# A transformer block: the preparation of cross attention placed inside self attention and the first cross steps

## What is computed

```python
attn_in = _adaln(x, cond, ln1_w, ln1_b, g1_w, g1_b, b1_w, b1_b)
x = _attn(attn_in, attn_in, sa_wq, sa_wkv, sa_wo, sa_bo) + x
cross_in = _adaln(x, cond, ln1_w, ln1_b, g1_w, g1_b, b1_w, b1_b)
ctx_n = _ln(context, ca_lnc_w, ca_lnc_b)
x = _attn(cross_in, ctx_n, ca_wq, ca_wkv, ca_wo, ca_bo) + x
```

## Time and profile before

| | us |
|---|---|
| median of 3 runs | 2244.72 (2241.64 to 2246.07) |
| the profiled execution | 2244.09 |
| its span, first to last instruction | 2242.2 |
| self attention, to the first transfer of `prepare` | 1555.25 |
| `prepare` and `project_context` | 90.07 |
| cross attention, from its first transfer at 1645.32 to its end at about 2037.3 | 392.0 |
| feed-forward | 204.9 |

### The profile page before, as it was taken

One profiled execution on the slowest core, in us unless ns is written; L12 is line 12 of the kernel. 1 busy time (PEld: TensorE's weight loads), 2 busy tenths in 40 slices (PEclk: granted clock), 3 DMA queues, 4 the chain that ended last, 5 costly groups with the idle time before them and its releaser, 6 DMA issues. The chain is left out here.

```text
span 2242.2 us, 40840 instructions
## 1 busy us (share of the span) xinstructions
PE 2056.6 (92%) x16376; PEld 932.5 (42%) x16376; DVE 1794.6 (80%) x2801; ACT 1378.4 (61%) x1748; POOL 35.0 (2%) x26
## 2 busy tenths in 40 slices
PE   4799999999999999999999999997379999986999
PEld 2233333345333335433333533335233444444676
DVE  5888999986899997799999689965768888844654
ACT  4577777765777766677677476762547666633442
POOL 1000000000000000000000000000400000000000
PEclk8799999999999999999999999998589999987999
DMA  5010101111110100111110111003323343324111
GB/s 189 29 39 30 48 30 58 40 39 42 55 39 30 67 37 23 61 45 39 39 39 30 48 59 38 30 20 97 91 81 116 111 124 125 120 73 130 38 39 38
DMA packets 102116, 136.04 MB, mean 61 GB/s; under 512 B 36694, under 2 KB 75176, under 8 KB 101928
## 3 DMA queue, kind: packets, MB, share of 16 engines
q1 hardware_dynamic: 101927, 133.43, 18.2%
HBM read 67.89 MB, written 13.11 MB: 36 GB/s over the span
## 5 line engine op out<-in xcount | busy, mean ns | idle before, releaser
L943 ACT ACTIVATE sa_probs<-sa_ps_s 128x1024 f32<-128x1024 f32 x512 | 496.3, 1021 | 216.1 <-PE sa_ps_s L734 216.1
L749 PE MATMUL sa_ps_o<-sa_probs,sa_v_pair 128*64 128x512 f32 x2048 | 530.9, 610 | 7.4 <-DVE sa_mx L1085 7.4
L1098 DVE TENSOR_TENSOR sa_acc<-sa_acc,sa_probs 128x1024 f32<-128x1024 f32 x384 | 452.7, 1220 | 16.5 <-ACT sa_probs L943 8.2
L1085 DVE CUSTOM_DVE_ANT_0 sa_rise<-sa_ps_t,sa_rise 128x512 f32<-128x512 f32 x504 | 327.1, 686 | 133.9 <-PE sa_ps_t L711 131.1
L931 ACT ACTIVATE sa_rise<-sa_ps_t 128x1024 f32<-128x1024 f32 x252 | 257.4, 1022 | 156.3 <-PE sa_ps_t L704 156.1
L727 PE MATMUL sa_ps_s<-sa_hi 64*128 64x512 f16 x1024 | 197.0, 377 | 0.9 <-ACT sa_raw L917 0.9
L727 PE MATMUL sa_ps_s<-sa_lo,sa_hi 64*128 64x512 f16 x1024 | 197.0, 377 | 0.0
L727 PE MATMUL sa_ps_s<-sa_hi,sa_lo 64*128 64x512 f16 x1024 | 196.8, 377 | 0.0
L749 PEld LDWEIGHTS sa_ps_o<-sa_probs,sa_v_pair 128*64 128x64 f32 x2048 | 114.7, 135 | 164.6 <-issue 96.4
L704 PE MATMUL sa_ps_t<-sa_kd,sa_hi 64*128 64x512 f16 x504 | 99.8, 390 | 33.2 <-ACT sa_raw L917 19.9
L704 PEld LDWEIGHTS sa_ps_t<-sa_kd,sa_hi 64*128 64x128 f16 x504 | 26.1, 93 | 216.6 <-issue 173.5
(11 more groups left out here) (329 smaller groups left out, 4020.7 us busy)
## 6 DMA issues: line engine op xcount, KB each, us to landing
sa_swp<-sa_raw SPq DMA_DIRECT2D x124, 256.0 KB, 2.4
sa_inv<-sa_scratch SPq DMA_DIRECT2D x128, 128.0 KB, 2.9
ca_swp<-ca_raw SPq DMA_DIRECT2D x64, 256.0 KB, 2.4
ca_inv<-ca_scratch SPq DMA_DIRECT2D x64, 256.0 KB, 3.9
sa_xs<-in_x SPq DMA_DIRECT2D x4, 1024.0 KB, 5.8
sa_xr<-in_x SPq DMA_DIRECT2D x4, 1024.0 KB, 5.8
cap_xs<-x_after_self SPq DMA_DIRECT2D x4, 1024.0 KB, 6.9
x_after_cross<-ca_xr SPq DMA_DIRECT2D x32, 128.0 KB, 2.0
```

What stands on the lines that cost most here:

```text
L749: ins = pe.matmul(ps_o[rows(x), half(c)], v_pair[:, kt, rows(x)], probs[:, kt % 2, c, half(x)], start=(kt == 0), stop=(kt == NK - 1))
L943: act.activation(probs[:, kt % 2, c, :], ps_s[c][:, :], ACT.Exp, scale=float(DH) ** -0.5).then_inc(s_p, 1)
L1085: dve.tensor_tensor_reduce(out=larger, in0=max_banks(j, t)[:, half(x)], in1=larger, scale=1.0, scalar=-3.0e38, op0=ALU.add, op1=ALU.max, a ...
L1098: dve.tensor_tensor(acc[:, c, :], before, probs[:, kt % 2, c, :], ALU.add).then_inc(s_acc[c], 1)
```

## The change

`prepare`, `project_context` and the function that clears semaphores are gone. Their work goes to four places.

- The loop of self attention: three more norms, u = 4, 5 and 6, for batches 0, 1 and 2 of x1, which are read back once they are stored. Norms 2 and 3 move to earlier steps. In the steps 30 and 31 and after the loop the cross weights are loaded into buffers that have come free (`later`) and converted (`following_high`, `following_low`).
- The beginning of self attention: the context is loaded, normalised, turned and split.
- The prologue of cross attention: `context_keys` and `context_values` on PE, `evacuate_keys`, `evacuate_values` and `high_keys` on ACT, `turned_keys` and `low_keys` on DVE.
- The first cross steps: the norm of batch 3, with statistics in steps 1 to 4, the inverse root in step 5, the normalising in steps 6 and 7 and the turning in steps 7 to 10.

The scale and shift (`gam`, `bet`) of self attention are kept and used again. `raw`, `hi`, `lo` and other buffers of the two attentions now share memory: `raw_or_keys` was `raw`, `scores_or_weights` holds `hi` and `lo` of self attention and then the cross weights, `context_or_sums` holds `cT` and then `sums`.

```diff
-def clear_semaphores(nc, sems):
...
-def prepare(nc, tag, consts, x_src, cond, norm, weights, xT_hi, xT_lo, context=None):
...
-def self_attention(nc, consts, x_src, x_dst, cond, norm, weights, bo, xT, wq, wk, wv, wo):
+def self_attention(nc, consts, x_src, x_dst, cond, norm, weights, bo, xT, wq, wk, wv, wo, shared, context, following):
...
-    NORMS = {1: (0, 1), 2: (8, 2), 3: (16, 3)}
+    NORMS = {1: (0, 1), 2: (5, 2), 3: (10, 3), 4: (16, 0), 5: (21, 1), 6: (28, 2)}
+    CROSS_NORMS = 4
...
+                if u >= CROSS_NORMS:
+                    sp.wait_ge(s_out, 16 * (norm_batch(u) + 1))
+                source = y_v if u >= CROSS_NORMS else x_v
+                sp.dma_start(xs[:], source[norm_batch(u)]).then_inc(s_nx, 16)
+            def stage_following(n):
+                src = following[n][0]
+                dst = later[n][0:src.shape[0]]
+                if len(src.shape) == 3:
+                    dst = dst.rearrange("p (a b) -> p a b", b=src.shape[2])
+                sp.dma_start(dst, src).then_inc(s_fw[n // 2], 16)
...
             sp.dma_start(ropeS[:], consts["sines"]).then_inc(s_rope, 16)
+            sp.dma_start(cs[:], c_src.rearrange("b m d -> m b d")).then_inc(s_c, 16)
+            sp.dma_start(crow[:, 0, :], c_w.partition_broadcast(M)).then_inc(s_c, 16)
+            sp.dma_start(crow[:, 1, :], c_b.partition_broadcast(M)).then_inc(s_c, 16)
                 swap(0, i)
+            sp.wait_ge(s_nlo, 4)
             stage(6)
             stage(7)
...
                     line(g + 1)
+                if g == G - 3:
+                    for i in (1, 0):
+                        sp.wait_ge(s_kq[i], 2 * G)
+                        for n in range(2):
+                            stage_following(2 * (1 - i) + n)
+                if g == G - 1:
+                    sp.wait_ge(s_v, 2 * G)
+                    for n in (4, 5):
+                        stage_following(n)
+                    sp.wait_ge(s_ntr, 4 * (len(NORMS) + 1))
+                    for n in (6, 7):
+                        stage_following(n)
...
+            def context_transposes():
+                pe.wait_ge(s_cn, 3)
+                for k, height, dst in c_parts:
+                    for b in range(B):
+                        ins = pe.transpose(dst[:, b * M:(b + 1) * M], cs[:, b, k * P:k * P + height], ident[0:M, 0:M])
+                    ins.then_inc(s_ct, 1)
...
+                if t == TT - 2:
+                    pe.wait_ge(s_kq_r[0], 4)
+                    context_transposes()
...
                     if norm_bank(g, kt) is not None:
                         u, n = norm_bank(g, kt)
                         pe.wait_ge(s_nxc, TT * (u + 1))
+                        if j == G:
+                            pe.wait_ge(s_v_r, 2 * G)
+                            pe.wait_ge(s_nxn, 4 * u + n)
                         transposes(u, n)
...
+                if t == 4:
+                    pe.wait_ge(s_nxn, 4 * (len(NORMS) + 1))
...
+            def following_high(n):
+                src, w_hi, _ = following[n]
+                height = src.shape[0]
+                act.wait_ge(s_fw[n // 2], 32)
+                act.activation(w_hi[0:height], later[n][0:height], ACT.Copy, scale=WS).then_inc(s_fhi, 1)
...
+            act.wait_ge(s_cst, 3)
+            act.activation(c_root[:], c_var[:], ACT.Sqrt).then_inc(s_croot, 1)
...
+                    if g == G - 2 and kt in (1, 3):
+                        if kt == 1:
+                            act.wait_ge(s_lo[0], G)
+                            act.wait_ge(s_lo[1], G)
+                        following_high(kt // 2)
...
+            act.wait_ge(s_st, NK * G)
+            for n in range(2, len(following)):
+                following_high(n)
...
+            context_variances()
             dve.wait_ge(s_rope, 32)
...
             weights_low(5)
+            context_norm()
             for t in range(TT):
...
                 rotated(1, i)
+            for n in range(2):
+                context_low(n)
             low(1, 1)
...
+                    if g == G - 2 and kt in (2, 4):
+                        n = kt // 2 - 1
+                        following_rest(n)
+                        following_low(n)
             reciprocals(G - 1)
+            dve.wait_ge(s_st, NK * G)
+            for n in range(2, 5):
+                following_rest(n)
+                following_low(n)
             for c in range(2):
...
-def project_context(nc, consts, cT, wk, wv, hi, lo, v_all):
...
-def cross_attention(nc, consts, x_src, x_dst, bo, xT, k_hi, k_lo, v_all, wq, wo):
...
+    STATS, NORMALISE, TRANSPOSE = range(1, 5), (6, 7), range(7, 11)
...
-            sp.dma_start(xr[:], x_v[0]).then_inc(s_x_first, 16)
             sp.wait_ge(s_blo, 1)
             sp.dma_start(bo_rows[1:2, :], bo_low[1:2, :]).then_inc(s_brow, 16)
+            for n in range(2):
+                sp.wait_ge(s_cev, PH * (n + 1))
+                sp.dma_start(k_half(k_swp, n)[0:P:2], k_half(k_raw, n)[1:P:2]).then_inc(s_kswap[n], 16)
+                sp.dma_start(k_half(k_swp, n)[1:P:2], k_half(k_raw, n)[0:P:2]).then_inc(s_kswap[n], 16)
             swap(0)
+            sp.dma_start(xs[:], x_v[LAST]).then_inc(s_nx, 16)
             swap(1)
+            sp.wait_ge(s_cpr, 2 * PAIRS)
+            sp.dma_start(xr[:], x_v[0]).then_inc(s_x_first, 16)
             for g in range(G):
                 if g + 2 < G:
                     swap(g + 2)
...
+            def context_keys(pair):
...
+            def context_values(n):
...
+            def transposes(n):
+                pe.wait_ge(s_nxc, TT if n else TT // 2)
...
+                if (b, pair, c) == (LAST, 0, 0):
+                    pe.wait_ge(s_nlo, 4)
...
+            for pair in range(PAIRS):
+                context_keys(pair)
             for j in range(3):
                 for c in range(2):
                     if j >= 1:
                         pe.wait_ge(s_q_r, 2 * (j - 1) + c + 1)
                     project(j, c)
+                if j == 1:
+                    for n in range(2 * B):
+                        context_values(n)
             pe.wait_ge(s_init, 4)
             pe.wait_ge(s_bo, 32)
+            pe.wait_ge(s_cev, 4 * PAIRS // 2)
+            pe.wait_ge(s_klo, 2)
             for g in range(G):
                 pe.wait_ge(s_hi, g + 1)
                 if g >= 1:
...
+                if g in TRANSPOSE:
+                    pe.wait_ge(s_sum_r, g - 1)
+                    transposes(TRANSPOSE.index(g))
                 pe.wait_ge(s_lo, g + 1)
                 scores(g)
                 if n is not None:
                     pe.wait_ge(s_yr, n + 1)
+                if g in TRANSPOSE:
+                    pe.wait_ge(s_nxn, TRANSPOSE.index(g) + 1)
                 if g >= 1:
                     if g >= 2:
                         pe.wait_ge(s_sum_r, g - 1)
...
+            def high_keys(n):
+                act.wait_ge(s_krot, n + 1)
+                act.activation(k_half(k_hi, n), k_half(k_raw, n), ACT.Copy).then_inc(s_khi, 1)
+            def inverse_root():
+                act.wait_ge(s_nst, len(STATS) + 2)
+                act.activation(newton[:], var[:], ACT.Ln).then_inc(s_nln, 1)
+                act.wait_ge(s_nln, 1)
+                act.activation(rstd[:], newton[:], ACT.Exp, scale=-0.5).then_inc(s_nln, 1)
...
+            def normalise(t):
+                act.wait_ge(s_nst, STEPS)
+                act.activation(xs[:, t, :], xs[:, t, :], ACT.Identity, bias=shift_x[:, t:t + 1],
+                               scale=rstd[:, t:t + 1]).then_inc(s_nxc, 1)
...
+            def norm_affine(n):
+                k = n // 2
+                act.wait_ge(s_ntr, n + 1)
+                act.wait_ge(s_nlo, n)
+                act.activation(xn[:], turn[0], ACT.Identity, bias=bet[:, k, LAST:B], scale=gam[:, k, LAST:B]).then_inc(s_nxn, 1)
...
+            def norm_high(n):
+                act.wait_ge(s_nxn, n + 1)
+                act.activation(norm_out(xT_hi, n), xn[:], ACT.Copy).then_inc(s_nhi, 1)
...
+            for pair in range(PAIRS):
+                evacuate_keys(pair)
             for j in range(2):
                 for c in range(2):
                     evacuate_q(j, c)
+            high_keys(0)
+            evacuate_values(0)
+            evacuate_values(1)
+            high_keys(1)
+            evacuate_values(2)
+            evacuate_values(3)
             high(0)
+            for n in range(4, 2 * B):
+                evacuate_values(n)
             high(1)
             for c in range(2):
                 evacuate_q(2, c)
...
+                if g in TRANSPOSE:
+                    norm_affine(TRANSPOSE.index(g))
                 if g >= 1:
                     evacuate_sums(g - 1)
                 for c in range(2):
                     exponentials(g, c)
+                if g in TRANSPOSE:
+                    norm_high(TRANSPOSE.index(g))
+                if g == STATS[-1] + 1:
+                    inverse_root()
+                if g in NORMALISE:
```

(26 more changed lines are left out.)

609 lines of the change are left out of this document (218 added, 391 removed).

## The result

The changed kernel takes 2210.64 us (median of four executions, 2206.14 to 2210.8), the kernel before, beside it, 2245.38 (2241.64 to 2246.07): a ratio of 0.9844, with a 95% interval of 0.9827 to 0.9861. That is 34.7 us less where 45.8 were forecast; 2210.64 lies inside the range of 2188 to 2213, above the forecast's own 2199 and near the rival of 2211. Faster had a chance of 0.97, and it is faster. The profiled execution took 2206.14 with a span of 2204.2, against 2244.09 and 2242.2: 38.0 between the two traces. What follows accounts for these 38.0; the median of after lies 4.5 above its own profiled execution, and that is taken up at the end.

What follows compares the result with a forecast made beforehand. No engine is full in the removed stages, a chain through five engines worth 90.07 us; PE fills plain self-attention steps, DVE's order sets cross steps 4 to 10. Added terms sum to 44.3, saving 45.8: 2199.0 us, range 2190 to 2212.

Steps and rivals of the forecast that it cites:

- choke rival: Cross steps 5 to 10 pay all added passes in series, 21 instead of 9.1, so 2211 us; chance 0.17.
- The prologue's chain: Cross attention, first transfer to first maxima: linked passes and swaps sum to 32.8 against 20.7 before, cost 12.1 us.
- nearer to the clean chain: Beginning of self attention: context norm costs 1.0 us, close to some 4.2 for its ten passes without GpSimd.
- the lock weighed there: Context norm: VectorE passes with two SBUF inputs and GpSimd instructions shut each other out; cost would be nearer to 3.
- normalising passes under ACT's 12.4 free: 0: Self attention: a norm's eight normalising passes of 0.595 on ACT lie under its free time and cost nothing.
- Weights in step 30: Self attention: converting two weight pieces, two DVE passes of 1.2 and a clearing, costs 1.0 us, bounds 0 and 3.
- End of self attention: After the last residual: the last three weight conversions outlast SP's wait for stores, cost 0.3 us, at most 3.5.
- the clock of the keys: Cross prologue: PE starts at its lower 1.2 GHz, so DVE's key work waits 6.5 plus 3.0 for a swap.
- Cross steps: Norm of batch 3 in cross attention's first steps costs 9.1 us, lower bound 5.1, upper 21.
- the rival with stalled switches: Table switches on ACT stall for as long again as the load, 2 x 1.28, so 2201.6 us; chance 0.03.
- The slower rival: New waits keep PE at 1.2 GHz in cross steps; about 5 lose the gain, 18 give near 2380; chance 0.02.
- Low clock past step 1: Cross attention: a low PE clock after step 1 in the profile was named as a sign of being wrong.

Runs made afterwards that it cites:

- all four together: Changed kernel plus weights in step 31, GpSimd behind context norm, own swap buffer for step 1, scaling first with spread normalising: 2194.64 us, ratio 0.9771.
- the second combination: Changed kernel plus weights in step 31, GpSimd behind context norm, own swap buffer for step 1, scaling first, no spreading: 2194.53 us, ratio 0.9774.

## Why the prediction was right and where it was off

**Right in the range, and in most of the mechanism.** 2210.64 lies near the top of the range, 11.6 above the forecast, and as a number it can't be told from the choke rival's 2211; the stretches tell them apart. Six of the seven terms came out too low, by 9.4 together, and only the prologue's, 1.5 too high, kept the sum from being further off. The removed 90.07 are gone and nothing behind them moved. Norm 6 measured 6.5 (5.9), and the plain price of a norm came back in every step where the trace of before had shown it. The prologue's chain was named link by link: DVE's wait of 1.60 for the shared buffer, no wait of the maxima for PE, the two halves of the keys ahead of everything. The cover at the end held: DVE still waited 3.26 for its transfer behind the three low halves.

**Beginning of self attention, 2.44 for 1.0.** Up to the first row it is 2.06 in this trace, and 1.5 to 2.8 over the nine traces. The step that failed is the choice "nearer to the clean chain". The row of `prepare` already showed 6.16 with GpSimd beside it, the lock weighed there would have given 3, and the norm took 7.6 here. With GpSimd out of the way the first row comes up to 0.7 earlier than before, so GpSimd's passes are the whole cost.

**Norms, 16.26 for 14.9.** The term "normalising passes under ACT's 12.4 free: 0" failed. It costs 0.45 in a plain step and 0.18 in an output step (64.84 in step 9 before, 64.66 in step 25). So norms 4 and 5 cost more than 7.45 each, and moving norms 2 and 3, costed at 0, cost 0.3 each, since their normalising left an output step for a plain one. Free time is a sum over a step; that the passes are paid because they stand ahead of a link of the ring is likely, and was not tested.

**Weights in step 30, 3.92 for 1.0.** The largest miss. It was costed by DVE's time in "a step with less DVE work"; the passes stand ahead of ACT's and DVE's links of the same ring, and ACT's two conversions (2.1) had no term at all. The bound of 3 held DVE's passes alone and was too low.

**End of self attention, 0.54 for 0.3.** From the last residual's end to the first transfer of what follows it took 3.69 instead of 3.29: the last low halves cost 0.40, for the forecast's 0.3. The other 0.14 lie ahead of the last residual, and their cause is open. One thing looks like a cost and is none. SP before, then after:

```profile
1535.06 0.33 SPq L591 DMA_DIRECT2D sa_scratch<-sa_few  x1
1536.46 2.40 SPq L595 DMA_DIRECT2D sa_inv<-sa_scratch  x4
```

```profile
1563.77 0.35 SPq L312 DMA_DIRECT2D sa_scratch<-sa_few  x1
1566.69 2.59 SPq L316 DMA_DIRECT2D sa_inv<-sa_scratch  x4
```

The first is issued and awaited before the second: 1.40 from one to the other before, 2.92 now, and from DVE's reciprocals to its division the path grew by 0.87 (7.28 to 8.15). But the last residual does not wait for it. In the eight traces with this end the division begins 50.7 to 51.2 after the last maxima, and the last residual ends at 60.3 in every one. Why the transfer takes longer is open; it took 1.43 without norm 6, with the same weights. The weights' last loads had landed over 7 us before it.

**Prologue, 10.56 for 12.1.** The term that missed is the clock of the keys. It was taken to be low throughout, as PE had stood idle. DVE's first pass on them came 8.4 after the first transfer, not 6.5 + 3.0 = 9.5; the rest of the chain took 22.9 for 23.3. The first 8 us in the changed kernel, then the first 8 us and the whole prologue in the one with GpSimd's wait, where this part of the program is the same:

```profile
1584.96:1592.96 8.00, 7.97 (x49) 5.27 (x50) 1.58 (x8) 3.30 (x9) 0.00 (x0) 0.82 0.22 87
```

```profile
1581.33:1589.33 8.00, 7.96 (x39) 4.92 (x40) 1.58 (x8) 2.54 (x7) 0.00 (x0) 0.62 0.05 15
1581.33:1614.13 32.80, 28.37 (x151) 15.37 (x153) 22.71 (x25) 15.65 (x28) 0.00 (x0) 0.86 0.38 137
```

At 0.62 the keys take 9.9 and the prologue the forecast's 32.8; in most traces with this chain the clock rises earlier and it takes 31.2 to 31.6. Behind the keys it is 22.8 to 22.9 in all of them.

**Cross steps, 11.85 for 9.1.** Step 4 measured +1.65 (1.6 forecast) and step 5 +1.36 (1.4). Step 5's inverse root is in these rows of ACT:

```profile
1666.04 1.92 ACT L1529 ACTIVATE ca_probs<-ca_ps_s 77x1024 f32<-77x1024 f32 x2
1667.97 1.28 ACT L1565 ACT_TABLE_LOAD   x1
1669.27 0.21 ACT L1565 ACTIVATE ca_newton<-ca_var 128x8 f32<-128x8 f32 x1
1669.49 1.28 ACT L1567 ACT_TABLE_LOAD   x1
1670.79 0.21 ACT L1567 ACTIVATE ca_rstd<-ca_newton 128x8 f32<-128x8 f32 x1
```

No switch costs more than its 1.28, here behind a full row of exponentials too; the rival with stalled switches is out. The Trainium skill, "ScalarE: Activation LUTs", section on what the load costs, adds a drain of 1.38 for each; the trace shows a gap of at most 0.02 on either side of a load.

Step 6 measured +1.02 for 0, and the clock did it: the step ran at 0.86, while in the kernel with the own swap buffer it ran at 0.97 and took 9.60, +0.1, and in the one with GpSimd's wait at 0.64 and took 12.17. But the dip had only moved: in the first of these two kernels step 5 ran at 0.68 and took 12.67. In every trace with this norm the steps 3 to 6 took 42.4 to 44.1 together, against 37.7 before and 37.7 without the norm. Steps 7 and 8 measured 2.62 and 2.55 for 1.0 and 3.1. The forecast put ACT's four passes of step 7 down as busy time over a free 2.86, but not where the scaling stands: behind a wait for DVE and ahead of a bank that PE needs. Moving it gave back 1.80 and 1.96. Step 3 cost 0.65, not 0, and this was a misreading: the 1.14 of the earlier trace rows stand ahead of the reduction in step 1, and "steps 1 to 3" took it for step 3 too. The reduction there had no wait ahead of it in the kernel before:

```profile
1698.34 1.43 DVE L1759 TENSOR_REDUCE ca_mx<-ca_ps_s 128x16 f32<-128x1232 f32 x1
```

In the steps 1 and 2 the statistics are free, as costed. Steps 9 and 10 measured 0.56 and 0.72 for 1.0 each, and step 0 took 0.61 more, at a clock of 0.71 instead of 0.75. So the rival "the cross steps choke" fell as a rule (21 for all passes in series), but the argument against it, ACT's 2.86 free per step, did not hold in the steps 7 and 8.

**The slower rival** was a clock that stays low. It never did: the steps 12 to 29 run at 0.99. But dips do come with the new waits. In the steps 3 to 10 before, one dip (0.83 in step 7) cost nothing, as DVE set the step; after, steps 4, 6 and 8 show 0.69, 0.86 and 0.86. "Low clock past step 1" had been named as a sign of being wrong, and in this form it came; the other two, a step over 48 and a prologue over 37, did not.

## What to carry to other kernels

An engine's free time in a step does not say what can be hidden in it: ask which instruction the new pass stands ahead of, and whether PE or another engine is waiting for that one. Work with no deadline (here weights, and the scaling of a turned tile) belongs behind a wait that the engine has anyway; two such moves gave 3.2 and 3.8 us net. Where GpSimd's passes run beside passes of VectorE whose operands all lie in SBUF, cost them one after the other; here that would have given 4.2 for the 3.6 that was paid.

## What the runs showed of the hardware

**PE's clock makes the same code take different times.** Step 0 of cross attention, the same instructions in the same order, took 8.14 to 10.74 in the traces (8.13 behind extra matmuls). Kernels with the own swap buffer, then all four together without the spreading, then with extra matmuls (step 0 of each):

```profile
1613.14:1623.88 10.74, 9.75 (x55) 3.27 (x57) 6.42 (x6) 4.83 (x8) 0.00 (x0) 0.68 0.19 76
...
1607.37:1615.51 8.14, 7.00 (x55) 2.73 (x56) 6.42 (x6) 4.71 (x8) 0.00 (x0) 1.00 0.25 101
...
1609.21:1617.34 8.13, 6.99 (x55) 2.72 (x56) 6.42 (x6) 4.71 (x8) 0.00 (x0) 1.00 0.25 101
```

The first two have the same prologue of 29.80 with the same idle time of PE at its end, and the clock (1.2 or 2.4 GHz, a mean of 0.68 or 1.00) fell in the one and not in the other. With matmuls in the gap it stayed up in both kernels that had them; without, in one of eleven traces of changed kernels. That the idle time lets it fall is likely, and not shown beyond that.

Step 30 of cross attention, which no experiment touches, in the changed kernel and in the second combination:

```profile
1938.03:1951.81 13.78, 11.50 (x75) 5.36 (x74) 5.29 (x7) 4.81 (x7) 0.00 (x0) 0.75 0.21 59
...
1923.38:1934.39 11.01, 8.68 (x75) 4.18 (x74) 5.81 (x7) 4.80 (x8) 0.00 (x0) 0.95 0.26 73
```

Twelve of the fourteen traces, that of the kernel before among them, have 13.7 to 13.8 there, two have 11.0.

The same step with the inverse root took 10.85 at a clock of 0.98 and 12.67 at 0.68; the prologue 31.2 to 31.6 or 32.6 to 32.8, and the first stretches of self attention 124.35 to 127.66. A few such places add up to several us. The executions of the changed kernel spread from 2206.14 to 2210.8 with mean clocks from 0.977 down to 0.972, those of the second combination from 2187.4 to 2197.5 with 0.982 down to 0.976. This is what would be expected, and may be the 4.5 between the profiled execution and the median of after; those executions have no trace, so it stays an argument. A forecast by terms can't be finer than this here.

**GpSimd's passes cost DVE nearly their own length.** The six passes of the context norm took 6.8 to 7.0 in nine traces with GpSimd beside them and 3.2 in four without, while GpSimd kept 4.2 to 4.4. Where in the group the time is lost depends on when GpSimd begins: its four small passes alone took 3.05 to 4.97.
